# Layer 0's edge sums of a four-layer graph network: a block for each tile of 128 edges, loads from two queues

## The chip, the cores and the metric

The kernel runs on one core of a Trainium2 chip. The metric is device time in microseconds (us) for the whole program, which is one launch; smaller is better. The core has five engines that run side by side and meet through semaphores: PE (TensorE, matmuls), DVE (VectorE), ACT (ScalarE), POOL (GpSimd) and SP (SyncE), which here only issues transfers.

## The reference

A graph has 6,250 nodes with 128 features and 200,000 edges sorted by their target `dst`. Four message-passing layers follow one another, each with a residual. The change touches only the edge sum of the first and the making of its lists:

```python
def _L0_gnn_ref(x, edge_index, W1, b1, W2, b2):
    src, dst = edge_index[0], edge_index[1]
    agg = jax.ops.segment_sum(x[src], dst, num_segments=6250)
    h = (1.0 + EPS) * x + agg
    return jax.nn.relu(h @ W1 + b1) @ W2 + b2
...
    x = x + _L0_gnn_ref(h, edge_index, L0_gnn_W1, L0_gnn_b1, L0_gnn_W2, L0_gnn_b2)
```

The targets are drawn as 6250 times the square of a uniform number, so that the first nodes have many more edges than the last. Layers 1 to 3 (a filter network with softplus, an attention layer with a segment softmax, a relation layer with another softmax) have edge stages of their own.

## The kernel before

Nodes are cut into 49 windows (`WIN`) of `P` = 128, edges into **groups** of `GE` = 512 = `KG` (4) tiles of 128. A group belongs to one window. The windows' edges fill at most `NG` = 440 groups, and all loops over groups run 440 times. Where a window's last group has fewer than 512 edges left, the rest of its tiles hold edges of the next windows, and their one-hot rows are zero.

**The lists.** `pack_edges` makes on DVE, for two orders of the edges, the window, the first edge and the base (128 times the window) of each group: counts per window, running sums (`scan`), and a comparison of each group's number with the running sums. SP writes the lists to DRAM and reads them back: `glist` (numbers) onto one partition, `gbase` broadcast to all, where DVE derives `gsame` (is this group's window that of the group before?).

**The edge sum of layer 0** is `segment_sums(k, 0)`, lines 1164 to 1320. For each group:

- SP `load`: waits on `summed`, reads the first edge's number (L1161), and loads the 512 edge records with one DMA of 128 partitions x 64 bytes (L1194). It leads the sum by one group (`LOAD` = 1).
- POOL `gather`: waits for the records and for `summed`, and issues four indirect DMAs (L1216); each fetches for 128 edges the source node's row as three bf16 parts, 768 bytes, into `sum_far`.
- DVE `one_hot`: the target within the window (L1233) and four one-hot tiles of 128x128 (L1237), one group ahead.
- PE `total`: 12 matmuls (L1301), four tiles by three parts, all accumulated into one block of 128x128 of PSUM bank a % 2. It waits for the one-hots, for the add of two groups before (two banks) and for the four gathers.
- DVE `add`: one operation (L1245) that takes the running block times `gsame` plus the bank's block.
- ACT `keep`: waits for the add, reads the window's number (L1157) and copies the running block to that window's place in `acc` (L1283); a later copy for the same window overwrites it.
- DVE `rank`: a piece of other work over 1,570 columns, one of four operations (L1251, L1254, L1258, L1261) in every second group.

Rows and gathered rows live in `U` = 4 slots, so that load and gather of group a wait until PE's sum of group a - 4 has been counted. Each engine runs its own instructions in program order; `skewed` writes that order, with the leads as offsets, in a loop of eight groups a turn. The semaphore `summed` is increased by PE's last matmul of a group, and `added` by the add, `kept` by the copy.

Later stages, which the change leaves alone, have the same shape with more work per group: the message sum (`sum_messages`), the attention stage (gathers at L1705) and the relation stage (gathers at L1943), all with eight slots and longer leads.

## Time and profile before

| what | us |
|---|---|
| median of three runs | 13527.47 |
| lowest and highest run | 13472.64, 13547.69 |
| the profiled execution, whole | 13520.75 |
| its span | 13518.5 |
| stage of layer 0's edge sums in it (269.0 to 3062.5) | 2793.5 |

The profile is one execution; starts are microseconds from the span's start. In rows of instructions, "[4.04 <-DMA x]" is the time that the engine was idle before the row and what its wait ended with. A name with q (SPq, ACTq) is the engine's sequencer, where transfers are issued and numbers read into registers; such instructions are not counted as busy. "issue" is idle time with nothing waited for. "remote" is a wait whose releaser the profile can't name. "x12" is the number of instructions in a row.

### The profile page before, as it was taken

How to read it: one execution, taken by the hardware profiler on the slowest of the kernel's cores; microseconds unless marked ns; L12 is line 12 of the kernel's file. 1: busy time of each engine (PE TensorE's matmuls, PEld its weight loads, DVE VectorE, ACT ScalarE, POOL GpSimd, SP SyncE). 2: the span in 40 equal slices, each digit the busy share in tenths (PEclk: the TensorE clock that was granted, in tenths of full speed). 3: DMA queues.
4: the chain of work that ended last, by engine and by line, in shares of the span. 5: the costliest groups of instructions: out<-in, count | busy, mean ns of one | idle time of the engine just before them, and what ended most of it. 6: DMA issues, size and time to landing. Idle time of an engine off the chain costs nothing. (4 is left out here: it accounts for less than half of the span.)

```text
span 13518.5 us, 245976 instructions
## 1 busy us (share of the span) xinstructions
PE 8019.6 (59%) x56223; PEld 6235.5 (46%) x56224; DVE 7891.0 (58%) x29629; ACT 4807.1 (36%) x9638; POOL 6957.0 (51%) x7329
## 2 busy tenths in 40 slices
PE   0222222226777767677885666666662878777776
PEld 0111111114444444444774655555552656555555
DVE  6333333335555555555776777777777666666665
ACT  2000000005555555555324555555552222222222
POOL 1656565553555555555214555555552555555553
PEclk9955555557676676666998888888886777777777
DMA  3222222221111111111651111111111222222221
GB/s 110 64 63 63 63 64 63 64 63 36 42 42 41 41 40 40 38 40 29 180 179 47 49 49 49 49 48 49 48 50 31 49 51 51 51 51 51 50 51 44
DMA packets 1025180, 771.96 MB, mean 57 GB/s; under 512 B 698606, under 2 KB 868943, under 8 KB 1024742
## 3 DMA queue, kind: packets, MB, share of 16 engines
q0 software_dynamic: 272816, 573.30, 15.3%
q1 hardware_dynamic: 752309, 198.07, 6.6%
q8 instruction: 18, 0.29, 0.0%
q14 instruction: 37, 0.30, 0.0%
HBM read 585.49 MB, written 155.84 MB: 55 GB/s over the span
## 5 line engine op out<-in xcount | busy, mean ns | idle before, releaser
L1492 POOL DMA_INDIRECT message_records<-f_msg,f_index x1760 | 1761.0, 1001 | 1683.8 <-DVE f_msg L1552 1162.7
L1705 POOL DMA_INDIRECT a_far<-node_table,a_rows x1784 | 1685.5, 945 | 1537.4 <-PE banks L1867 479.5
L1943 POOL DMA_INDIRECT r_far<-node_table,r_rows x1784 | 1704.4, 955 | 1467.9 <-remote 505.4
L1216 POOL DMA_INDIRECT sum_far<-split_table,sum_rows x1760 | 1668.8, 948 | 1205.1 <-issue 625.9
L1301 PE MATMUL banks<-sum_far,sum_hot 128*128 128x128 bf16 x5280 | 627.3, 309 | 2252.5 <-DVE sum_hot L1237 1260.2
L1301 PEld LDWEIGHTS banks<-sum_far,sum_hot 128*128 128x128 bf16 x5280 | 528.7, 143 | 2351.0 <-issue 1345.6
L1245 DVE SCALAR_TENSOR_TENSOR sum_cur<-sum_cur,gsame,banks 128x128 f32<-128x128 f32 x440 | 151.7, 345 | 1805.9 <-remote 1376.6
L1532 DVE SCALAR_TENSOR_TENSOR f_soft<-f_pos_part,f_logs 128x512 f32<-128x512 f32 x442 | 304.5, 689 | 1401.5 <-remote 763.9
L1283 ACT ACTIVATE acc<-sum_cur 128x128 f32 x440 | 136.1, 309 | 2704.8 <-DVE sum_cur L1245 1853.0
L1620 PE MATMUL banks<-f_attr_t,w_f 20*128 20x512 f32 x890 | 722.0, 902 | 560.7 <-ACT f_attr_t L1564 278.8
L1612 PE MATMUL banks<-w_W_f,f_soft 128*128 128x128 f32 x3528 | 757.3, 357 | 239.3 <-issue 236.9
L2032 ACT ACTIVATE r_keys<-banks 128x1024 bf16<-128x1024 f32 x446 | 455.2, 1021 | 1056.6 <-remote 886.3
L2072 PE MATMUL banks<-near,r_hot_t 128*128 x5328 | 767.0, 257 | 81.4 <-issue 70.5
L1564 ACT ACTIVATE f_attr_t<-banks 20x512 f32<-20x512 f32 x446 | 260.3, 584 | 1523.5 <-remote 1353.1
L1859 PE MATMUL banks<-ident,a_prob_t 128*128 128x128 f32 x1768 | 325.3, 312 | 798.7 <-ACT a_prob_t L1811 788.5
L2091 PE MATMUL banks<-r_far,r_share 128*128 128x129 f32 x3528 | 718.7, 362 | 120.7 <-DVE r_share L2010 69.9
L1612 PEld LDWEIGHTS banks<-w_W_f,f_soft 128*128 128x128 f32 x3528 | 640.3, 259 | 277.0 <-issue 275.5
L2091 PEld LDWEIGHTS banks<-r_far,r_share 128*128 128x128 f32 x3528 | 604.9, 257 | 158.8 <-DVE r_share L2010 86.0
L1867 PE MATMUL banks<-a_far,a_prob 128*128 128x129 f32 x3528 | 621.8, 332 | 84.2 <-ACT a_prob L1789 71.0
L1632 PE MATMUL banks<-near,f_hot_t 128*128 x5292 | 563.2, 272 | 151.1 <-issue 145.2
L1806 ACT ACTIVATE a_keys<-banks 128x512 bf16<-128x512 f32 x446 | 266.3, 597 | 1026.9 <-remote 585.2
L1867 PEld LDWEIGHTS banks<-a_far,a_prob 128*128 128x128 f32 x3528 | 560.7, 241 | 127.7 <-ACT a_prob L1789 78.4
(350 smaller groups left out, 21274.5 us busy)
## 6 DMA issues: line engine op xcount, KB each, us to landing
m_rows<-message_records SPq DMA_DIRECT2D x223, 264.0 KB
m_rows<-message_records POOLq DMA_DIRECT2D x223, 264.0 KB
acc<-a_cur SPq DMA_DIRECT2D x440, 65.0 KB
acc<-r_cur SPq DMA_DIRECT2D x440, 65.0 KB
a_far<-node_table,a_rows POOLq DMA_INDIRECT x1784
r_far<-node_table,r_rows POOLq DMA_INDIRECT x1784
sum_far<-split_table,sum_rows POOLq DMA_INDIRECT x1760
message_records<-f_msg,f_index POOLq DMA_INDIRECT x1760
```

Of the source, the lines that this page charges most:

```text
L1216: pool.indirect_dma_start(far[:, u, q, :], None, k.table3[:, :], bass.IndirectOffsetOnAxis(ap=rows[:, u, q, C_SRC:C_SRC + 1].bitcast(I32), ...
L1301: last = nc.tensor.matmul(k.psum[a % 2][:, 0:D], hot[:, u, q, :], rhs, start=q == 0 and part == 0, stop=q == KG - 1 and part == (2 if o == ...
L1492: pool.indirect_dma_start(k.mrec[:, :], bass.IndirectOffsetOnAxis(ap=index[:, u, q:q + 1], axis=0), msg[:, u, q, :], None, bounds_check=ED ...
L1612: last = nc.tensor.matmul(filter_ps[b][:, q * D:(q + 1) * D], soft[:, b, q * P:(q + 1) * P], w_f2[:, :], start=True, stop=True)
L1620: nc.tensor.matmul(hidden_ps[b], k.w_f1[:, :], attr_t[:, b, :], start=True, stop=True).then_inc(hidden_ready, 1)
L1632: last = nc.tensor.matmul(ps[:, q * D:(q + 1) * D], hot_t[:, q * P:(q + 1) * P], k.near[:, w, part * D:(part + 1) * D] .rearrange("p a d - ...
L1705: pool.indirect_dma_start(far[:, u, q, 0:D], None, k.table[:, :], bass.IndirectOffsetOnAxis(ap=rows[:, u, q, C_SRC:C_SRC + 1].bitcast(I32) ...
L1867: last = nc.tensor.matmul(sum_ps[b][:, 0:D + 1], prob[:, b, q * P:(q + 1) * P], far[:, u, q, 0:D + 1], start=q == 0, stop=q == KG - 1)
L1943: pool.indirect_dma_start(far[:, u, q, 0:D], None, k.table[:, :], bass.IndirectOffsetOnAxis(ap=rows[:, u, q, M_DST - M_SRC:M_DST - M_SRC + ...
L2032: nc.scalar.activation(keys[:, a % 2, :, :], key_ps, ACT.Copy).then_inc(keys_taken, 1)
L2072: nc.tensor.matmul(near_ps[b][:, span], hot_t[:, h, span], k.near[:, w, part * D:(part + 1) * D] .rearrange("p a d -> p (a d)"), start=par ...
L2091: last = nc.tensor.matmul(sum_ps[b][:, 0:D + 1], share[:, b, q, :], far[:, u, q, 0:D + 1], start=q == 0, stop=q == KG - 1)
```

## The change

Layer 0 gets a function of its own, `sum_targets`, in place of `segment_sums(k, 0)`. Its unit is the **tile** of 128 edges of one window: at most `NT` = 1612 tiles, each with its own window, first edge and base. Four tiles in a row of the list make a group, whatever their windows, so there are `NTG` = 403 groups. The lists are made in `pack_edges` with some 30 more linked DVE operations of the same kinds, go out in three more DMAs, and are read at the start of the stage: the numbers onto one partition, the base as [128, 1664] broadcast, from which DVE makes `same`.

- Slots for rows and gathered rows: `S` = 8 in place of 4; the gathered rows lie in memory of a later stage (`k.near`). One-hots keep four slots. Leads: loads 7, gathers 4, one-hots 2, sums 1, adds 0 (before: 1, 0, 1, 0, 0).
- SP loads tiles 0 and 1 of a group, ACT tiles 2 and 3: four DMAs of 128 partitions x 16 bytes (L1235) in place of one.
- PE puts each tile's three matmuls into a block of its own of the bank, 12 per group as before.
- DVE chains four adds per group (L1306), each waiting for the last through `carried`.
- ACT copies four blocks per group to `acc` (L1350), with four window numbers read (L1232). In its loop, the load of group a + 7 (which waits for the sum of a - 1) stands ahead of the copies of group a.
- `skewed` takes `total`, with the three groups that are no whole turn of eight written out behind the loop.

```diff
+NT = EDGES // P + WIN + 1
+NTG = (NT + KG - 1) // KG
+TQ = 13
+NTL = P * TQ
...
+                dve.wait_ge(numbered, 2)
...
+                upto = scan(dve, groups, WIN)
+                link(dve, nc.vector.tensor_tensor(tpast[:, :, :], ti[:, :].unsqueeze(2).to_broadcast(spread),
+                                                  upto[:, 0:WIN].unsqueeze(1).to_broadcast(spread), ALU.is_ge))
+                link(dve, nc.vector.tensor_reduce(tw[:, :], tpast[:, :, :], AX, ALU.add))
...
+                sp.wait_ge(listed, 1)
+                for i, t in enumerate((tw_i, ts_i)):
+                    sp.dma_start(k.tile_lists[i, :].rearrange("(p q) -> p q", p=P), t[:, :]).then_inc(list_out, 16)
+                sp.dma_start(k.tile_bases[0, :].rearrange("(p q) -> p q", p=P), tb[:, :]).then_inc(list_out, 16)
...
-def skewed(eng, *stages, counts=None, turn=U):
+def skewed(eng, *stages, counts=None, turn=U, total=NG):
...
+    whole = total // turn * turn
+    with eng.Fori(0, whole, turn) as g:
         if counts:
             counts.turn()
         for u in range(turn):
             for lead, stage in stages:
                 stage(g, u + lead)
+    for n in range(whole, total):
+        for lead, stage in stages:
+            stage(0, n + lead)
...
-    LOAD, HOT, SUM, ADD = 1, 1, 0, 0
...
+    LOAD, GATHER, HOT, SUM, ADD = 7, 4, 2, 1, 0
+    S, H = 2 * U, U
...
+        far = k.near[:, 0:S * KG, :].rearrange("p (u q) c -> p u q c", q=KG)
...
+        def numbers(eng, which, g, a, first, n, most):
+            place = tiles[0:1, which, bass.ds((g + a) * KG + first, n)]
+            return nc.values_load_multi_w_load_instructions(place, engines=[eng.engine], min_val=0, max_val=most)[1]
+
+        def load_tile(eng, e0, u, q):
+            eng.dma_start(rows[:, u, q, :], k.erec[bass.ds(e0, P), :]).then_inc(loads_in[u], 16)
...
+                sp.dma_start(tiles[:, :, :], k.tile_lists.rearrange("(a i) g -> a i g", a=1)).then_inc(listed, 16)
+                sp.dma_start(base[:, :], k.tile_bases.broadcast_to([P, NTL])).then_inc(listed, 16)
+                sp.wait_ge(listed, 32)
...
                 def load(g, a):
-                    sp.wait_ge(summed, now(g, s_sum + a + 1))
-                    e0 = first_edge(sp, k, o, g + a)
-                    sp.dma_start(rows[:, a % U, :, :].rearrange("p q c -> p (q c)"),
-                                 records[bass.ds(e0, GE), :].rearrange("(p q) c -> p (q c)", q=KG))\
-                        .then_inc(k.rows_in[a % U], 16)
-                skewed(sp, (LOAD, load), counts=now, turn=2 * U)
...
+                    wait(sp, now, summed, g, a, S)
+                    sp.sem_inc(k.loading, 1)
+                    for q, e0 in enumerate(numbers(sp, 1, g, a, 0, 2, EDGES + EP)):
+                        load_tile(sp, e0, a % S, q)
+                skewed(sp, (LOAD, load), counts=now, turn=S, total=NTG)
...
+                    pool.wait_ge(loads_in[u], slot_count(now, g, a, 16 * KG, S, s_load[u]))
+                    wait(pool, now, summed, g, a, S)
+                    pool.sem_inc(k.begun, 1)
+                    for q in range(KG):
+                        pool.indirect_dma_start(
+                            far[:, u, q, :], None, k.table3[:, :],
+                            bass.IndirectOffsetOnAxis(ap=rows[:, u, q, C_SRC:C_SRC + 1].bitcast(I32), axis=0))\
+                            .then_inc(gathered[u], 16)
+                skewed(pool, (GATHER, gather), counts=now, turn=S, total=NTG)
...
+                    dve.wait_ge(loads_in[u], slot_count(now, g, a, 16 * KG, S, s_load[u]))
+                    wait(dve, now, summed, g, a, H)
+                    nc.vector.tensor_tensor(rel[:, h, :], rows[:, u, :, C_DST].bitcast(I32), base[:, bass.ds((g + a) * KG, KG)],
...
-                    dve.wait_ge(summed, now(g, s_sum + U + a + 1))
-                    dve.wait_ge(added, now(g, s_add + 2 + a))
-                    dve.wait_ge(kept, now(g, s_kept + a + 1))
-                    nc.vector.scalar_tensor_tensor(cur[:, u, :], cur[:, (u - 1) % U, :], k.gsame[o][:, bass.ds(g + a, 1)],
-                                                   k.psum[a % 2][:, 0:D], ALU.mult, ALU.add).then_inc(added, 1)
+                    wait(dve, now, summed, g, a)
+                    dve.wait_ge(kept, now(g, KG * (a + 1), KG))
+                    for q in range(KG):
+                        past = cur[:, u, q - 1, :] if q else cur[:, (u - 1) % U, KG - 1, :]
+                        dve.wait_ge(chained, now(g, KG * a + q + 1, KG))
+                        last = nc.vector.scalar_tensor_tensor(cur[:, u, q, :], past, same[:, bass.ds((g + a) * KG + q, 1)],
+                                                              k.psum[a % 2][:, q * D:(q + 1) * D], ALU.mult, ALU.add)
+                        last.then_inc(chained, 1)
+                    dve.wait_ge(chained, now(g, KG * a + KG + 1, KG))
+                    dve.sem_inc(added, 1)
...
+                act.wait_ge(listed, 32)
+                act.sem_inc(kept, KG * U)
+
+                def load(g, a):
+                    wait(act, now, summed, g, a, S)
+                    act.sem_inc(k.loading, 1)
+                    for q, e0 in enumerate(numbers(act, 1, g, a, 2, 2, EDGES + EP)):
+                        load_tile(act, e0, a % S, 2 + q)
 
                 def keep(g, a):
-                    act.wait_ge(added, now(g, s_add + 2 + a + 1))
+                    wait(act, now, added, g, a)
                     act.sem_inc(k.loading, 1)
-                    act.wait_ge(kept, now(g, s_kept + U + a))
-                    act.sem_inc(k.loading, 1)
-                    w = window(act, k, o, g + a)
-                    nc.scalar.activation(k.acc[:, w, 0:D], cur[:, a % U, :].unsqueeze(1), ACT.Copy).then_inc(kept, 1)
-                skewed(act, (ADD, keep), counts=now, turn=2 * U)
+                    for q, w in enumerate(numbers(act, 0, g, a, 0, KG, WIN)):
+                        act.wait_ge(kept, now(g, KG * U + KG * a + q, KG))
+                        nc.scalar.activation(k.acc[:, bass.ds(w, 1), 0:D], cur[:, a % U, q, :].unsqueeze(1), ACT.Copy).then_inc(kept, 1)
+                skewed(act, (LOAD, load), (ADD, keep), counts=now, turn=S, total=NTG)
...
                 def total(g, a):
-                    u = a % U
-                    pe.wait_ge(onehot_ready, now(g, s_hot + a + 1))
-                    pe.wait_ge(added, now(g, s_add + a + 1))
-                    if o == 0:
-                        pe.wait_ge(k.pool_done[u], now(g, s_pool[u] + 16 * KG * (a // U + 1), 16 * KG // U))
+                    u = a % S
+                    wait(pe, now, onehot_ready, g, a)
+                    wait(pe, now, added, g, a, 2)
+                    pe.wait_ge(gathered[u], slot_count(now, g, a, 16 * KG, S, s_gather[u]))
                     for q in range(KG):
-                        for part in range(3 if o == 0 else 1):
-                            rhs = far[:, u, q, part * D:(part + 1) * D] if o == 0 else rows[:, u, q, 0:D]
-                            last = nc.tensor.matmul(k.psum[a % 2][:, 0:D], hot[:, u, q, :], rhs,
-                                                    start=q == 0 and part == 0, stop=q == KG - 1 and part == (2 if o == 0 else 0))
+                        for part in range(3):
+                            last = nc.tensor.matmul(k.psum[a % 2][:, q * D:(q + 1) * D], hot[:, a % H, q, :],
+                                                    far[:, u, q, part * D:(part + 1) * D], start=part == 0, stop=part == 2)
                     last.then_inc(summed, 1)
-                skewed(pe, (SUM, total), counts=now, turn=2 * U)
+                skewed(pe, (SUM, total), counts=now, turn=S, total=NTG)
```

ACT's program in one pass of the loop. Before, one copy of `sum_cur` into `acc` for each group:

```order
L1280 REGISTER_ALU [waits added]
L1157 ISA [waits kept]
L1157 TENSOR_LOAD glist
L1157 ISA x2
L1283 ISA
L1283 ACTIVATE acc<-sum_cur 128x128
```

Now, for each group, from the load of two tiles' records (`t_rows`) to the second of the four copies:

```order
L1232 ISA [waits summed]
L1232 TENSOR_LOAD t_tiles
L1232 ISA x4
L1235 ISA
L1235 DMA t_rows<-edge_records 128x4
L1235 ISA
L1235 DMA t_rows<-edge_records 128x4
L1163 REGISTER_ALU
L1232 ISA [waits added]
L1232 TENSOR_LOAD t_tiles
L1232 ISA x8
L1349 REGISTER_ALU
L1350 ISA [waits kept]
L1350 ACTIVATE acc<-t_cur 128x128
L1349 REGISTER_ALU
L1350 ISA [waits kept]
L1350 ACTIVATE acc<-t_cur 128x128
```

ACT now waits for two semaphores in turn, `summed` for the load and `added` for the copies, and issues two DMAs per group where it issued none.

DVE's program at the head of the loop. Before, from the one-hots of one group to its add:

```order
L1232 REGISTER_ALU [waits rows_in1]
L1233 ISA [waits summed]
L1233 TENSOR_SCALAR sum_rel<-sum_rows,gbase 128x4
L1237 TENSOR_SCALAR sum_hot<-iota_b,sum_rel 128x128 [waits rel_ready]
L1237 TENSOR_SCALAR sum_hot<-iota_b,sum_rel 128x128 x3
L1242 REGISTER_ALU
L1245 REGISTER_ALU [waits kept,added,summed]
L1245 SCALAR_TENSOR_TENSOR sum_cur<-sum_cur,gsame,banks 128x128
```

Now, the adds of one group, behind the same five operations for the one-hots:

```order
L1302 ISA [waits summed]
L1305 REGISTER_ALU [waits kept]
L1306 ISA [waits carried]
L1306 SCALAR_TENSOR_TENSOR t_cur<-t_cur,t_same,banks 128x128
L1305 REGISTER_ALU
L1306 ISA [waits carried]
L1306 SCALAR_TENSOR_TENSOR t_cur<-t_cur,t_same,banks 128x128
L1305 REGISTER_ALU
L1306 ISA [waits carried]
L1306 SCALAR_TENSOR_TENSOR t_cur<-t_cur,t_same,banks 128x128
L1306 ISA [waits carried]
L1306 SCALAR_TENSOR_TENSOR t_cur<-t_cur,t_same,banks 128x128
```

One add of 128x128 has become four, in a chain.

## Rows read from the trace of the kernel before

**Rows 1.** The page: busy tenths of POOL in 40 slices of the span
```profile
POOL 1656565553555555555214555555552555555553
```
**Rows 2.** Busy time in stretches: us, then PE, PEld, DVE, ACT, POOL (count), PEclk, DMA, GB/s
```profile
269.00:3062.50 2793.50, 627.32 (x5280) 528.74 (x5280) 960.61 (x2870) 136.10 (x440) 1668.78 (x1760) 0.59 0.25 64
...
7226.00:10233.00 3007.00, 1991.66 (x16197) 1781.77 (x16195) 2183.41 (x8316) 1671.57 (x4379) 1654.38 (x1752) 0.86 0.19 49
10487.00:13406.00 2919.00, 2318.73 (x16635) 1719.24 (x16633) 1837.94 (x10074) 852.46 (x1749) 1674.18 (x1752) 0.73 0.22 51
```
**Rows 3.** One line's instructions, POOL's gathers (L1216): duration, and what ended idle time
```profile
L1216 POOL DMA_INDIRECT sum_far<-split_table,sum_rows x1760: 940/947/1295, 272.7 to 3048.8; - x196
...
  issue: 625.9, 1651
  DMA sum_rows<-edge_records: 419.3, 74
  PE banks L1301: 152.3, 33
  remote: 7.6, 2
```
**Rows 4.** Timeline of layer 0's stage from 1548 to 1563 us, all engines
```profile
1548.28 1.44 PE L1301 MATMUL banks<-sum_far,sum_hot 128*128 128x128 bf16 x12 [3.65 <-DMA sum_far<-split_table,sum_rows]
...
1555.52 0.95 POOL L1216 DMA_INDIRECT sum_far<-split_table,sum_rows  x1 [0.30 <-issue]
1559.41 0.35 DVE L1245 SCALAR_TENSOR_TENSOR sum_cur<-sum_cur,gsame,banks 128x128 f32<-128x128 f32 x1 [12.43 <-remote]
...
1560.72 0.31 ACT L1283 ACTIVATE acc<-sum_cur 128x128 f32 x1 [13.75 <-DVE sum_cur L1245]
1561.13 0.34 DVE L1245 SCALAR_TENSOR_TENSOR sum_cur<-sum_cur,gsame,banks 128x128 f32<-128x128 f32 x1
...
1562.51 0.95 POOL L1216 DMA_INDIRECT sum_far<-split_table,sum_rows  x1 [6.04 <-DMA sum_rows<-edge_records]
```
**Rows 5.** Count of matmuls (L1301) from the stage's start to 1559.00: us, PE, PEld
```profile
269.00:1559.00 1290.00, 287.67 (x2424) 242.58 (x2424) 0.69 0.25 64
```
**Rows 6.** Count of DVE's adds (L1245) in the same stretch: us, DVE
```profile
269.00:1559.00 1290.00, 69.00 (x200) 0.69 0.25 64
```
**Rows 7.** One line's instructions, DVE's add (L1245): what ended DVE's idle time before it
```profile
  remote: 1376.6, 144
```
**Rows 8.** Timeline at the start of the attention stage, POOL and DVE
```profile
7212.79 0.94 POOL L1705 DMA_INDIRECT a_far<-node_table,a_rows  x1 [0.30 <-issue]
...
7216.85 0.70 DVE L1740 TENSOR_TENSOR banks<-banks,a_far 128x512 f32<-128x512 f32 x1 [30.41 <-remote]
...
7226.75 0.94 POOL L1705 DMA_INDIRECT a_far<-node_table,a_rows  x1 [13.01 <-PE banks L1867]
```
**Rows 9.** Instructions of sequencers and ACT's copy: duration min/median/max in ns
```profile
L1194 SPq DMA_DIRECT2D sum_rows<-edge_records x441: 4/333/1397, 270.0 to 3045.6; - x147
...
L1157 ACTq FUSED_REGOPS  x1760: 42/100/173, 283.2 to 7015.5; - x196
...
L1157 ACTq TENSOR_LOAD <-glist x880: 272/279/492, 283.3 to 7015.1; - x176
...
L1283 ACT ACTIVATE acc<-sum_cur x440: 309/309/311, 284.2 to 3056.8; 128x128 f32 x147
```
**Rows 10.** Timeline of the stage's first loads and first gather
```profile
270.00 4.29 SPq L1194 DMA_DIRECT2D sum_rows<-edge_records  x4
...
272.68 1.14 POOL L1216 DMA_INDIRECT sum_far<-split_table,sum_rows  x1 [96.78 <-issue]
```
**Rows 11.** The lists: DVE's operations for one of them, and the load of `gbase` (timeline)
```profile
149.90:158.96 9.06, 0.00 (x0) 0.00 (x0) 7.78 (x39) 0.00 (x0) 0.00 (x0) 1.00 0.02 1
...
162.12 0.34 SPq L478 DMA_DIRECT2D gbase<-group_bases  x1
165.63 0.06 DVE L464 MEMSET gsame<- 128x1 f32 x1 [6.68 <-DMA gbase<-group_bases]
```

More of the change, by code:

```diff
@@ L245, in program @@
         publish(k, k.hs, True)
-        segment_sums(k, 0)
+        sum_targets(k)
         sum_nodes(k)
@@ new lines, in load @@
+                    wait(sp, now, summed, g, a, S)
[3 more added lines that the diff above has]
+                skewed(sp, (LOAD, load), counts=now, turn=S, total=NTG)
+                sp.wait_ge(pos_ready, 1)
+                for half in range(2):
+                    sp.dma_start(k.epos[half * EP:(half + 1) * EP, :].rearrange("(p j) a -> p (j a)", p=P), pos_i[:, :])\
+                        .then_inc(pos_out, 16)
@@ new lines, in _, with gather @@
+                sp.wait_ge(pos_out, 32)
+                for u in range(S):
+                    sp.wait_ge(loads_in[u], s_load[u] + len(range(u, NTG + LOAD, S)) * 16 * KG)
+            @block.gpsimd
+            def _(pool):
+                now = Counts(pool)
+                def gather(g, a):
+                    u = a % S
[8 more added lines that the diff above has]
+                skewed(pool, (GATHER, gather), counts=now, turn=S, total=NTG)
@@ L1222, in _ @@
             @block.vector
             def _(dve):
[L1224 to L1225 removed]
                 now = Counts(dve)
[L1229 to L1235 removed]
+                k.link(dve, nc.vector.memset(cur[:, :, :, :], 0.0))
@@ L1303, in total @@
                     last.then_inc(summed, 1)
-                skewed(pe, (SUM, total), counts=now, turn=2 * U)
-    k.since.passed(NG + HOT, rel_ready, onehot_ready)
-    k.since.passed(NG + U, summed, kept)
-    k.since.passed(NG + 2, added)
-    per_slot(k.since, k.rows_in, 16, LOAD)
-    if o == 0:
-        per_slot(k.since, k.pool_done, 16 * KG, 0)
+                skewed(pe, (SUM, total), counts=now, turn=S, total=NTG)
+    for u in range(S):
+        k.since.passed(16 * KG * len(range(u, NTG + LOAD, S)), loads_in[u])
+        k.since.passed(16 * KG * len(range(u, NTG + GATHER, S)), gathered[u])
```

124 lines of the change are left out of this document (62 added, 62 removed).

## The prediction

> **What bounds the kernel now.** I read the slices first: the change touches layer 0's edge sums, in which POOL is the busiest engine for a fifth of the span [rows 1]. The table of stretches puts that stage at 2793.5 us, with POOL busy for 1668.8, DVE for 960.6, PE for 627.3 and ACT for 136.1 [rows 2]. So no engine is full, and the question is what POOL waits for. Its own line answers: 1,760 gathers of 0.95 us, and between them 625.9 us of "issue", of which 96.8 precede the first gather [rows 3, 10]; the remaining 529 us over 440 groups are 1.20 us per group. Four gathers take 4 x 0.95 + 1.20 = 5.0 us. On top POOL waits 419.3 us for the records, 152.3 for the banks and 7.6 for others: 579 us in 109 pauses, 5.3 us each and one per 4.04 groups [rows 3]. 440 x 5.0 + 579 = 2779, which with the start and the end is the stage.
>
> **Why POOL pauses** is the main reading. The timeline shows PE finishing a group's matmuls at 1548.28 + 1.44 = 1549.72 [rows 4]. DVE's add for it, which waits only for that and for an add and a copy long done, starts at 1561.13, and the add of the group before at 1559.41 [rows 4]. The counts agree: at 1559.00 PE had run 2,424 matmuls, 202 groups of 12, and DVE 200 adds [rows 5, 6]. So the increment that PE's last matmul makes reaches the others up to 10 us late. In the stretch POOL starts its last gather at 1555.52 and ends it at 1556.47; then comes 2.9 us of nothing, DVE's add, and at 1562.51 POOL again, after 6.04 us [rows 4]. The attention stage starts the same way: POOL gathers without a break until 7213.7, DVE's wait of 30.41 us ends at 7216.85, 3.1 us behind the last gather, and POOL goes on at 7226.75, after 13.01 us, though its slots are eight [rows 8]. DVE waited 1376.6 us for "remote" before its add, 144 times [rows 7]: a releaser that left no record in time. My reading: while gathers follow one another at 1.25 us, PE's increments are held back; when POOL runs out of slots, they arrive after about 3 us; then records are loaded and the next run begins. Before, a run is 4.04 groups, the four slots, and a pause is 5.3 us.
>
> Where the profile gives an end time to a matmul, the Trainium skill (Perfetto Trace Analysis, section on the Tensor Engine instruction) warns that it is an estimate, and that the semaphore goes out only when PSUM has acknowledged. By that rule the 10 us could be PSUM's; that the increment then comes about 3 us behind POOL's last gather, twice, speaks for POOL. The sum is the same by either.
>
> **The change, part by part.**
>
> *Fewer groups.* 403 for 440 in the loop; POOL also gathers the 4 ahead of it, 407 in all. With nothing but this, 33 x 6.31 (= 2776 from the first gather to the last, over 440) = 208 us less.
>
> *Deeper slots.* A run of gathers was bounded by 4 slots and can now be up to 8 groups. It doesn't reach 8 for sure: PE waits for the add two groups back, the adds wait for the late increments, so at the end of a run up to six gathered groups have not been summed, and their slots come free one after another, while POOL has started again. Bounds: 4.04 as now, and 8. I take 6.5, above the middle, since some increments also come within a run.
>
> *The pause* has a new chain behind it. The increment arrives 3 us after the last gather as now; since longer runs hold more of them (the wait in the attention stage ended after 3.1 us with 8 slots [rows 8]), I allow 3 to 5. Then:
> - SP's half of the records: about 1.4 us for a list read and two issues (0.33 us each [rows 9], and up to 1.4 where a row is stretched), and 272.68 - 270.00 - 0.33 = 2.35 us from the end of an issue to POOL's start [rows 10]. With the increment 6.8 to 8.8 us.
> - ACT's half stands behind the copies of the last group in its order. Those wait for four adds, 4 x 0.35 + the waits between = 1.7 us; then for a read of four numbers (0.28 + four times some 0.25 of register work, from 0.10 per operation [rows 9]) and four copies of 0.31 [rows 9] with a wait after each, together 3.3 us. Between add and copy one number took 1560.72 - 1559.41 - 0.35 = 0.96 us [rows 4], so this isn't too much. Then 1.4 us of issues and 2.35: 3 + 1.7 + 3.3 + 1.4 + 2.35 = 11.8, up to 13.8.
>
> Before, the same sum was 2.9 + 3.1 = 6.04 in the example and 5.3 on average, since some pauses start with an increment on its way. When several increments arrive together ACT's later loads do hide behind gathers, so I take 9.5, between SP's path and ACT's. That is 9.5 / 6.5 = 1.46 us per group where it was 5.3 / 4.04 = 1.31.
>
> *PE.* 12 matmuls per group as before, 1.44 us [rows 4], under POOL's 5.0. *DVE.* It was 960.6 / 440 = 2.18 us per group [rows 2]; three more adds of 0.35 and their waits make 3.6, under POOL. If POOL's cover were gone (all waits away), DVE would still fit. *ACT.* One copy and one number become 3.3 + 1.4 + waits = 5.1 us per group, just over POOL's 5.0 and under my pace; nothing is hidden there for long, see below.
>
> *Start and lists.* Making the tile lists: another set like the 39 operations of 9.06 us [rows 11], on the path, +9. At the stage's start a broadcast load 3.6 times as wide as `gbase`, which took 165.63 - 162.12 = 3.5 us [rows 11], bound 3.5 to 12.6, and a comparison on DVE: I take +6. The clearing of `acc` on DVE is beside the first gathers. Three list DMAs and POOL's second `iota`: below 1 us.
>
> **Sum.** Pace 5.0 + 1.46 = 6.46 us. 407 x 6.46 = 2629, + 4 from the stage's start to the first gather as before + 6 for the loads, and nothing at the end, since the last four groups gathered are never summed: 2639. Against 2793.5 that is -154; with the lists +9, **-145**. The profiled execution was 13520.75, so 13,376; the median lies 6.7 above it: 13,383 us. I say **13,380**. Its own range: pace 6.2 to 6.87 (the attention stage's 3007 / 438 [rows 2], where the same eight slots stand over twice the DVE work) gives 407 x -0.26 = -106 and 407 x +0.41 = +167, so 13,275 to 13,550.
>
> **Rivals.**
>
> *A: the eight slots swallow the late increments.* Within a run some increments do come, or POOL would never get beyond its slots; if they come at least every 10 us, eight slots never run dry. Then POOL is the bound, 407 x 5.0 = 2035 + 27 for start and end = 2062; -731 + 9: 12,805 us. With a residual of 0.6 per group 13,050. For it: 109 pauses, each one as the four slots ran out. Against it: the attention stage and the relation stage, with eight slots, hold 6.87 and 6.66 us [rows 2], and DVE's 30 us without an increment [rows 8]. But their groups carry 5.0 us (2183 / 438) and 4.2 us of DVE and 4.5 and 5.3 us of PE, so part of that pace is their own.
>
> *B, the slower side: ACT is held back as SP is.* SP's instructions, a 0.33 us issue for one, take up to 1.4 us [rows 9] in this stage, and ACT's do not (0.49 at most), but ACT issued no DMA here. If it is the issuing that exposes a sequencer, ACT's 5.1 us get longer: 4 of its 29 sequencer instructions per group held by one step of 0.65 us make it 5.1 + 2.6 = 7.7. Then ACT is the bound for every group: 407 x 7.7 = 3134 + 10; +350 + 9: 13,887 us. It decides from about 6.85 us of ACT per group on, where 407 x 6.85 meets the old stage.
>
> *C: the small loads queue.* The stage's first four loads took 4.29 us, (4.29 - 0.33) / 3 = 1.3 us apart with a number read for each [rows 10]. If four DMAs of one group come in at that distance, a pause grows by 3 x 1.3 = 4.0, or 0.61 per group: pace 7.07, +248: 13,630. Two issuers speak against the full price. The Trainium skill (DMA: Bandwidth & Descriptors, Rules for kernel authors) tells to coalesce, as below 64 KB one pays mostly overhead, and says in Issuing engines are not separate DMA queues that two engines only save issue time. By that rule the four transfers of 2 KB cost more than the one of 8 KB, which is this rival; no row of before has loads from two queues here.
>
> That the loop isn't shortened at all can be left out: its length is a constant, 403.
>
> **Chances.** Main .50, A .25, B .13, C .12. A measurement here tells about 0.5%, 67 us, from no change. Faster by more than that, below 13,460: A, and .35 of main: .60. Within: .12 of main and .05 of C: .17. Slower: B, .07 of C, .03 of main: .23. The range takes in A at 12,805 and C, and leaves out B: 12,800 to 13,750.
>
> **What would show it.** In the profile after: the stage's length near 2640; some 60 pauses of POOL of 9 to 10 us, each some 6.5 groups apart, ending with the records and not with the banks (if pauses are fewer than 20, A). DVE's add starting 3 to 5 us after POOL's last gather, with matmuls long done. ACT's issues as the last loads of a group before POOL restarts; ACT's issue rows with a median of 0.35 us or less (if they reach 0.7 to 1.4, B). The four loads of a group landing within 1 us of their issues (if they land 1.3 apart, C). I am wrong as a whole if PE's increments are late for a reason that isn't POOL, such as the load on the banks: three accumulations per block in place of twelve would then change the lateness itself.

## The result, and the profile after

The changed kernel took 13,692.55 us at a median of four runs (13,688.97 to 13,706.16), the kernel before beside it 13,529.56 (13,472.64 to 13,547.69): a ratio of 1.013, 95% interval 1.0099 to 1.016. I had forecast 13,380, faster. The time lies inside the stated range; the sign is wrong.

One thing must be known to read the numbers below: the same kernel before, run beside the experiments, took 10,374 to 10,385 us on six occasions and 13,502 and 13,665 us on two others; two of the chips showed both. I call them the **prompt** and the **late** condition, by what the traces show to differ between them. The result, and the profile on which the prediction was made, are late. In the late condition whole times also drift: the kernel before took 13,473 to 13,665 us.

The page of the changed kernel, late: POOL's busy tenths over the span (as rows 1).

```profile
POOL 1555555553555555555323555555552555555553
```

The stage of layer 0 in the same kernel: us, then busy PE, PEld, DVE, ACT, POOL (count), PEclk, DMA share, GB/s (as rows 2).

```profile
275.00:3198.00 2923.00, 583.06 (x4848) 484.73 (x4848) 1316.78 (x3845) 498.38 (x1612) 1547.56 (x1628) 1.00 0.25 57
```

The stage took 2923.0 us where it was 2793.5: +129.5. The stretch ahead of it is 6.0 longer (lists), the rest of the kernel, which is unchanged, took 10,506.5 against 10,456.0, +50.5; together 186, the difference of the two spans. The last part is within what this kernel varies between runs; the first two are the change. PE's granted clock was full in the stage (1.00, 2.4 GHz) where it had been 0.59 on average, mostly at the lower level of 1.2 GHz, and the stage was longer all the same: PE was no bound before or after.

POOL's gathers (L1269), what ended its idle time (as rows 3):

```profile
L1269 POOL DMA_INDIRECT near<-split_table,t_rows x1628: 942/949/2067, 285.1 to 3184.3; - x181
its engine sat idle before it (us, times) until:
  DMA t_rows<-edge_records: 904.7, 184
  issue: 493.5, 1416
  PE banks L1365: 56.2, 28
```

(2899.2 us over 1,627 intervals: 7.13 us per group.) Taking off the 101.8 us ahead of the first gather, POOL waited 859 us in 211 pauses of 4.1 us, one per 1.9 groups. Before it was 109 pauses of 5.3, one per 4.0 [rows 3]. So pauses became twice as frequent, where I had forecast fewer. They end with the records, as I had said. DVE's adds tell who is late now. DVE's add (L1306), what ended DVE's idle time before it (as rows 7):

```profile
  ACT acc L1350: 1179.6, 334
```

DVE may not overwrite a slot of the running block before ACT has copied it, four groups on. It waited for ACT for 1,180 us, where before it waited for no copy at all. ACT itself hardly waited: what ended its idle time before its copies (L1350) was almost always nothing at all.

```profile
  issue: 2219.3, 426
```

Counting instruction by instruction, ACT's sequencer stood for 81 of 2,899 us in front of its semaphore waits, and SP's for 1,280. So ACT had become the pace. The timeline of two groups in the middle of the stage:

```profile
1546.94 1.61 ACT L1350 ACTIVATE acc<-t_cur 128x128 f32 x4 [3.56 <-issue]
...
1551.20 0.95 POOL L1269 DMA_INDIRECT near<-split_table,t_rows  x1 [0.30 <-issue]
...
1553.49 0.84 ACTq L1235 DMA_DIRECT2D t_rows<-edge_records  x2
1556.05 1.61 ACT L1350 ACTIVATE acc<-t_cur 128x128 f32 x4 [7.49 <-issue]
1556.68 0.95 POOL L1269 DMA_INDIRECT near<-split_table,t_rows  x1 [4.53 <-DMA t_rows<-edge_records]
1557.79 1.82 DVE L1306 SCALAR_TENSOR_TENSOR t_cur<-t_cur,t_same,banks 128x128 f32<-128x128 f32 x4 [4.42 <-ACT acc L1350]
```

Between two sets of copies ACT issues two loads; POOL restarts 3.2 us after the first of them, DVE adds when the four copies that began at 1556.05 are done. What ACT does between 1549.13 and 1553.49 is the heart of the matter. These are its sequencer's instructions (start and duration in us, from the trace):

```
1549.13 0.015 EVENT_SEMAPHORE (summed)
1549.15 0.013 FUSED_REGOPS
1549.19 0.704 TENSOR_LOAD t_tiles
1550.59 0.015 FUSED_REGOPS
1550.61 0.015 SEQ_ASSERT
1552.02 0.018 FUSED_REGOPS
1552.04 0.707 SEQ_ASSERT
1553.44 0.006 FUSED_REGOPS
1553.49 0.334 DMA_DIRECT2D t_rows
```

An assert that takes 0.018 us elsewhere takes 0.707, and register operations stand 1.41 us apart. POOL's last gather ran from 1551.20 to 1552.15, and from 1553.44 on ACT's instructions have their usual lengths again. From the first gather to the last, 727 of ACT's 13,471 sequencer instructions took over 0.6 us; in the kernel before, none of 3,658.

### The profile page after: what moved, and what is told of

Same layout as the page of the kernel before. It is cut to its first block and busy times, and to the rows that moved or that the text cites. A ratio compares the mean times of both kernels' runs of the same rounds, so it can differ in the third digit from the quotient of the medians.

```text
span 13704.5 us, 262447 instructions
## 1 busy us (share of the span) xinstructions
PE 7988.4 (58%) x55791; PEld 6205.3 (45%) x55792; DVE 8249.8 (60%) x30630; ACT 5172.2 (38%) x10810; POOL 6831.9 (50%) x7198
## 5 line engine op out<-in xcount | busy, mean ns | idle before, releaser
L1269 POOL DMA_INDIRECT near<-split_table,t_rows x1628 | 1547.6, 951 | 1454.4 <-DMA t_rows<-edge_records 904.7
L1365 PE MATMUL banks<-near,t_hot 128*128 128x128 bf16 x4848 | 583.1, 309 | 2409.1 <-DVEq L1310 1643.4
L1365 PEld LDWEIGHTS banks<-near,t_hot 128*128 128x128 bf16 x4848 | 484.7, 142 | 2507.4 <-issue 2503.6
L1350 ACT ACTIVATE acc<-t_cur 128x128 f32 x1612 | 498.4, 309 | 2475.6 <-issue 2219.3
L1306 DVE SCALAR_TENSOR_TENSOR t_cur<-t_cur,t_same,banks 128x128 f32<-128x128 f32 x1612 | 559.7, 347 | 1423.7 <-ACT acc L1350 1179.6
L2098 ACT ACTIVATE banks<-banks 128x512 f32<-128x512 f32 x444 | 260.4, 586 | 933.9 <-remote 821.2
```

The costliest lines, as they stand in the source:

```text
L1269: pool.indirect_dma_start(far[:, u, q, :], None, k.table3[:, :], bass.IndirectOffsetOnAxis(ap=rows[:, u, q, C_SRC:C_SRC + 1].bitcast(I32), ...
L1306: last = nc.vector.scalar_tensor_tensor(cur[:, u, q, :], past, same[:, bass.ds((g + a) * KG + q, 1)], k.psum[a % 2][:, q * D:(q + 1) * D], ...
L1350: nc.scalar.activation(k.acc[:, bass.ds(w, 1), 0:D], cur[:, a % U, q, :].unsqueeze(1), ACT.Copy).then_inc(kept, 1)
L1365: last = nc.tensor.matmul(k.psum[a % 2][:, q * D:(q + 1) * D], hot[:, a % H, q, :], far[:, u, q, part * D:(part + 1) * D], start=part == 0 ...
```

## The experiments

Nine kernels, four of them met in both conditions. Runs of the same kernel are told together. The table gives each run and the kernel before that was measured beside it; "per group" is POOL's mean distance between gathers, times four; "long" is the number of sequencer instructions over 0.6 us from the first gather to the last.

| kernel | condition | us | before | per group | long SP / ACT |
|---|---|---|---|---|---|
| before | late | 13,521 | | 6.31 | 554 / 0 |
| changed | late | 13,693 | 13,530 | 7.13 | 631 / 727 |
| one load on ACT (g2) | late | 13,584 | 13,502 | 6.86 | 1095 / 949 |
| all loads on SP (i3) | late | 13,791 | 13,665 | 7.02 | 1094 / 862 |
| one-window groups, 8 slots (j1) | late | 13,688 | 13,665 | 6.27 | 647 / 528 |
| before (f1) | prompt | 10,377 | 10,383 | 5.01 | 0 / 0 |
| changed (f2) | prompt | 10,308 | 10,383 | 5.19 | 1 / 1 |
| two gathers left out (g1) | prompt | 10,309 | 10,378 | 5.19 | 1 / 1 |
| all loads on SP (e1) | prompt | 10,237 | 10,382 | 5.02 | 1 / 0 |
| one copy (e3) | prompt | 10,237 | 10,382 | 5.02 | 0 / 1 |
| one-window groups, 8 slots (e5) | prompt | 10,421 | 10,382 | 5.02 | 0 / 0 |
| the same, load on ACT (h3) | prompt | 10,426 | 10,377 | 5.02 | - / 0 |
| before, load on ACT (e2) | prompt | 11,028 | 10,382 | 6.48 | - / 0 |

(g1 has two gathers to a group: 2108.7 us over 406.5 groups. The first row is the profiled execution of the median 13,527. "Changed, late", e1 and e5 are medians of four, four and five runs, with their intervals in the text; all other rows are single runs. The 13,665 beside i3 and j1 is one and the same execution.)

As whole times drift in the late condition, the stretch from the first gather to the last is the firmer number there, though it too is one trace each: 2776.1 us before, 2899.2 changed, 2789.2 in g2, 2855.1 in i3, 2783.5 in j1.

### All loads on SP

```diff
-                    for q, e0 in enumerate(numbers(sp, 1, g, a, 0, 2, EDGES + EP)):
+                    for q, e0 in enumerate(numbers(sp, 1, g, a, 0, KG, EDGES + EP)):
...
-                skewed(act, (LOAD, load), (ADD, keep), counts=now, turn=S, total=NTG)
+                skewed(act, (ADD, keep), counts=now, turn=S, total=NTG)
```

> The changed kernel with all four tile loads of a group issued by SP; ACT only copies. Theory 1 (ACT, once it issues transfers, is held back in steps of 0.7 and 1.4 us while POOL gathers, and its 7.2 us per group are the pace): ACT's sequencer rows in layer 0's stage have no step of 0.7 us any more, the pace falls to 5.8 to 6.6 us per group, time 13,230 to 13,520 us. Theory 2 (the four copies and four numbers per group are too much for ACT's place in the chain, whoever issues the loads): the pace stays near 7.2 us, time 13,650 to 13,720 us. A third outcome, slower than 13,720 us, would say that SP with four issues per group is held back even more.

> As before for this kernel. Beside a kernel before of 13,500 us: no steps among ACT's instructions and 13,470 to 13,560 us by theory 1; above 13,650 us if SP is the one held.

The first runs were in the prompt condition: 10,237 against 10,382, ratio 0.9864 (0.9848 to 0.9881), four runs; repeats gave 10,239, 10,239, 10,245 and 10,235. There POOL gathers without a pause:

```profile
L1269 POOL DMA_INDIRECT near<-split_table,t_rows x1628: 942/946/2155, 286.3 to 2328.6; - x181
its engine sat idle before it (us, times) until:
  issue: 495.3, 1626
```

In the late condition (i3) the same kernel took 13,791 against 13,665, one run each: slower by 126 us, and 79 us more than before from the first gather to the last. "Above 13,650 if SP is the one held" came true. DVE's one-hots (L1292) show it; the first row is how often and for how long DVE waited for records, the others SP's and ACT's durations for the numbers (L1232), min/median/max in ns:

```profile
  DMA t_rows<-edge_records: 1199.9, 367
```

```profile
L1232 SPq FUSED_REGOPS  x2040: 2/147/1402, 281.1 to 3144.6; - x186
L1232 ACTq FUSED_REGOPS  x2012: 3/147/997, 299.6 to 3126.2; - x183
L1232 SPq SEQ_ASSERT  x1640: 2/18/1392, 281.3 to 3144.8; - x183
L1232 ACTq SEQ_ASSERT  x1612: 3/18/727, 300.5 to 3127.0; - x180
```

One pass of SP for four loads takes 3.6 us undisturbed and took 10.3 in the middle of a run of gathers (1548.26 to 1558.52). SP's sequencer stood for 5 of 2,855 us in front of its waits, ACT's for 623: here SP was the pace. And ACT, which issues no transfer in this kernel, still has 862 long instructions. **Theory 1, that issuing transfers is what exposes ACT, has fallen.**

### One load on ACT, three on SP

> The changed kernel with three of a group's loads on SP and one on ACT in place of two and two. ACT's undisturbed pass gets shorter by one number (0.17 us) and one issue (0.52 us), from 5.14 to 4.45 us, under POOL's 5.0. Beside a kernel before of 10,380 us: if ACT's pass is the bound and nothing else of the two-queue form costs anything, 10,235 to 10,245 us, as with all loads on SP. Beside 13,520 us: by theory 1 ACT is still held in steps while it issues at all, pace 6.3 to 6.9 us, 13,330 to 13,570 us; all loads on SP would do better than that.

This run was in the late condition: 13,584 against 13,502. Its pace of 6.86 us is in the range I gave, its time 14 us above the upper end, and all loads on SP did not do better, as I had expected, but worse. By the paces, the two-and-two split is the slowest (7.13), three-and-one the least slow (6.86), all on SP between (7.02). Of 2,789 us ACT's sequencer stood for 156 in front of its waits and SP's for 605, so ACT was still the slower one. Work moved from one held sequencer to the other; no split brings the pace near 6.31.

### The kernels before and after, again

> The kernel before, unchanged, for its profile beside the next three. In the first profile it took 13,521 us; beside the four experiments so far it took 10,382 us at a median, 23% less. Two theories of that gap. Theory 3 (late increments): what differs is only whether PE's increments and the sequencers' steps come late while POOL gathers; where they do, layer 0's stage has 109 to 116 pauses and takes about 2,794 us, where they don't it has none and takes 440 x 5.02 = 2,209 us plus 15. Theory 4 (clock or memory speed): single operations, POOL's gathers of 0.95 us or the matmuls, have other durations. The total will be near 13,520 or near 10,380 us; nothing between, by theory 3.

> The changed kernel, unchanged. Theory 3: where PE's increments are late (the kernel before near 13,520 us), 13,690 us as measured first; where they are not (before near 10,380 us), ACT fits under POOL, the 33 groups fewer give 33 x 5.02 = 166 us back less 9 for the lists and some 12 at the start: 10,225 to 10,250 us, faster than before by 1.3%. If ACT were too slow for its place whatever the increments do, it would be slower than before in both.

f1 came out as theory 3 had it: no pause in layer 0's stage, single gathers of the same length (a median of 946 ns against 947). The stage is 576 us of the 3,143 between the two conditions; the other 2,566 lie behind it, in stages whose pace I have not taken apart. The stage of f1 (as rows 2) and what ended POOL's idle time in it:

```profile
268.00:2485.50 2217.50, 635.32 (x5280) 527.82 (x5280) 968.03 (x2871) 136.06 (x440) 1667.66 (x1760) 1.00 0.31 80
```

```profile
L1216 POOL DMA_INDIRECT sum_far<-split_table,sum_rows x1760: 942/946/1141, 271.6 to 2474.2; - x196
its engine sat idle before it (us, times) until:
  issue: 632.8, 1760
```

PE's increments were not late either: 0.02 us after the modelled end of the matmul at most. In the late trace an increment's record lies up to 10.4 us behind the latest matmul end before it, which is a lower bound, as two increments can arrive together: matmuls that ended at 1544.63 and 1549.72 were followed by increments at 1559.30 and 1559.42. So four slots are enough where nothing is held. The changed kernel was faster there, by 0.7%, but 58 us above the upper end of what I expected. Its ACT, in two passes of the loop with nothing held (f2):

```profile
1002.05 1.61 ACT L1350 ACTIVATE acc<-t_cur 128x128 f32 x4 [3.65 <-PE banks L1365]
...
1003.79 1.82 DVE L1306 SCALAR_TENSOR_TENSOR t_cur<-t_cur,t_same,banks 128x128 f32<-128x128 f32 x4 [2.09 <-ACT acc L1350]
1004.66 0.85 ACTq L1235 DMA_DIRECT2D t_rows<-edge_records  x2
...
1007.19 1.61 ACT L1350 ACTIVATE acc<-t_cur 128x128 f32 x4 [3.52 <-issue]
```

From copies to copies it is 5.14 us with no wait in it, and POOL needs 5.01. ACT's sequencer didn't stand in front of a wait for over 0.12 us once between the first gather and the last, in f2 as in g1 below.

### Two gathers left out

```diff
-                    for q in range(KG):
+                    for q in range(2):
                         pool.indirect_dma_start(
...
-                                                    far[:, u, q, part * D:(part + 1) * D], start=part == 0, stop=part == 2)
+                                                    far[:, u, q % 2, part * D:(part + 1) * D], start=part == 0, stop=part == 2)
```

> The changed kernel with two of POOL's four gathers per group left out (PE multiplies the one-hots of tiles 2 and 3 with the rows of tiles 0 and 1). ACT's program is untouched. POOL then needs 2.5 us per group and can't be the bound. If ACT's own row of instructions is what sets the pace (5.14 us per group read between two passes of its loop where nothing is late), the pace stays at 5.15 to 5.3 us and the time, beside a kernel before of 10,380 us, is 10,290 to 10,320 us, as with four gathers (10,308). If POOL's gathers were the bound there, the stage falls by up to half: below 10,000 us. Beside a kernel before of 13,520 us: if ACT's steps of 0.7 us come from POOL's gathers, half of them are gone, pace 5.3 to 6.3 us; if they have another source, it stays at 7.2.

10,309.3 against 10,308.4 with all four gathers, one run each: POOL's work was halved and the time didn't move. In the prompt condition ACT's pass sets the changed kernel's pace, not POOL's gathers. The run was not in the late condition, so that half of the expectation stays untried.

### One copy per group

```diff
-                    for q, w in enumerate(numbers(act, 0, g, a, 0, KG, WIN)):
-                        act.wait_ge(kept, now(g, KG * U + KG * a + q, KG))
...
+                    for q, w in enumerate(numbers(act, 0, g, a, KG - 1, 1, WIN)):
+                        act.wait_ge(kept, now(g, U + a))
```

> The changed kernel with one copy and one window number per group on ACT in place of four (copies of tiles 0 to 2 are left out); its two loads per group stay. Theory 1: ACT stays held back, but has some 2 us less to do per group: the pace falls from 7.2 to 5.8 to 6.6 us, time 13,130 to 13,500 us, with the steps of 0.7 us still in ACT's rows. Theory 2: the pace falls as well, but to POOL's and the slots' bound, 5.0 to 5.6 us, below 13,100 us.

> The changed kernel with one copy and one number per group on ACT in place of four (copies of tiles 0 to 2 left out), its two loads kept. Beside 13,500 us: theory 1 expects the steps to stay and the pace to fall from 7.2 to 5.8 to 6.5 us, 13,130 to 13,420 us, since ACT has 10 instructions fewer that can be held. If the four copies are what counts, not the holding, no steps are needed to explain it and the time is below 13,100. Beside 10,380 us: 10,237 us.

Both runs (e3, h4) were in the prompt condition, 10,237 and 10,239 us, the time of all loads on SP. Either way of shortening ACT's pass below POOL's 5.0 gives back the same 70 us. Of the late condition these runs say nothing, and the two theories of the expectations were about that alone.

### Groups of one window with eight slots

The load, one-hot, add and copy of the kernel before, 440 groups, with the changed kernel's slots, leads and semaphores.

```diff
-                    for q, e0 in enumerate(numbers(sp, 1, g, a, 0, 2, EDGES + EP)):
-                        load_tile(sp, e0, a % S, q)
-                skewed(sp, (LOAD, load), counts=now, turn=S, total=NTG)
+                    e0 = first_edge(sp, k, 0, g + a)
+                    sp.dma_start(rows[:, a % S, :, :].rearrange("p q c -> p (q c)"),
+                                 k.erec[bass.ds(e0, GE), :].rearrange("(p q) c -> p (q c)", q=KG)).then_inc(loads_in[a % S], 16)
+                skewed(sp, (LOAD, load), counts=now, turn=S, total=NG)
```

> Groups of 512 edges of one window, one load by SP, one add and one copy per group as in the kernel before (440 groups), but with the eight slots and the leads 7, 4, 2, 1, 0 of the changed kernel; the tile lists are still made (9 us). It shows what slots and leads alone do. If eight slots swallow PE's late increments (rival A of the prediction), POOL is the bound with 5.0 to 5.3 us per group: 12,960 to 13,090 us. If pauses stay as in the main forecast, 5.3 us each for 6.5 groups, 5.8 us per group: 13,290 to 13,380 us. If deeper slots change nothing, 13,500 to 13,560 us.

> Groups of one window, eight slots, long leads, one load by SP. Beside a kernel before of 13,500 us: SP has 7 instructions per group that can be held in place of the changed kernel's 17 on SP and 29 on ACT. If the number of SP's and ACT's instructions is what made the changed kernel slow, this one has pauses no oftener than before: 13,290 to 13,400 us if longer runs save pauses, 13,480 to 13,560 if they don't. If it lies above 13,650 too, the eight slots themselves do harm. Beside 10,380 us: 10,421 us, nothing new.

Prompt (e5): 10,421 against 10,382, ratio 1.004 (1.0026 to 1.0054), and 10,424 and 10,421 in repeats. Of the 39 us the lists are 9, and four groups gathered ahead that nobody sums 20 (16 gathers of 1.25 us); some 10 are not accounted for. The three outcomes of the expectation all presumed the late condition, so this run decided none of them.

Late (j1): 13,688 us, one run; the nearest kernel before is the 13,665 measured beside i3. From the first gather to the last it is 2783.5 us against 2776.1, with four groups more gathered. **Eight slots with the long leads gain nothing by themselves.** POOL's gathers:

```profile
L1267 POOL DMA_INDIRECT near<-split_table,t_rows x1776: 940/946/1345, 279.3 to 3062.8; - x198
its engine sat idle before it (us, times) until:
  issue: 524.6, 1676
  DMA t_rows<-edge_records: 489.4, 65
  PE banks L1348: 148.3, 26
  remote: 30.9, 9
```

Counted in one way for both (gaps of over 2.2 us between starts, less the 1.25 of a gather): 99 pauses of 5.61 us, 555 us, where the kernel before had 116 of 4.92, 571 us. Runs got longer and pauses longer with them. The timeline shows such a run:

```profile
1542.16 0.34 DVE L1298 SCALAR_TENSOR_TENSOR t_cur<-t_cur,gsame,banks 128x128 f32<-128x128 f32 x1
...
1558.14 0.35 DVE L1298 SCALAR_TENSOR_TENSOR t_cur<-t_cur,gsame,banks 128x128 f32<-128x128 f32 x1 [12.88 <-issue]
1558.59 1.44 PE L1348 MATMUL banks<-near,t_hot 128*128 128x128 bf16 x12 [14.45 <-issue]
...
1565.33 0.35 DVE L1298 SCALAR_TENSOR_TENSOR t_cur<-t_cur,gsame,banks 128x128 f32<-128x128 f32 x1 [5.88 <-remote]
1565.49 0.94 POOL L1267 DMA_INDIRECT near<-split_table,t_rows  x1 [3.97 <-remote]
```

PE stands still for 14.45 us, since it may be only two groups ahead of the adds and the adds wait for its increments. While POOL works through its slots nothing else moves, so the groups gathered meanwhile have all to be summed afterwards, and the slots come free at PE's and DVE's pace. ACT, with one copy and one number per group and no transfer, has 528 long instructions, against none in the kernel before, whose ACT program is nearly the same. But it is no bound here: its sequencer stood for some 1,630 of 2,783 us in front of its waits, and SP's for 1,370.

### The load on ACT, with four and with eight slots

```diff
-                skewed(act, (ADD, keep), counts=now, turn=2 * U)
+                skewed(act, *(((LOAD, load),) if o == 0 else ()), (ADD, keep), counts=now, turn=2 * U)
```

> The kernel before, with the one load per group of layer 0 issued by ACT ahead of its copy in place of by SP; nothing else. Theory 1: ACT's list reads and register operations, which never took over 0.5 us before, are now spread by steps of 0.7 and 1.4 us, some hundreds of them in the stage; as ACT has little to do per group, the time moves by less than 1%, 13,450 to 13,650 us. Theory 2: no such steps in ACT's rows, time 13,470 to 13,550 us.

> The same as the last, with the group's one load issued by ACT ahead of its copy. ACT's undisturbed pass is 2.6 us per group, far under POOL's 5.0. Beside 13,500 us: theory 1 expects hundreds of steps of 0.7 and 1.4 us among ACT's instructions, which hardly show without the load; the time moves by less than 60 us, as 2.6 us leave room. If ACT has no steps, theory 1 falls. Beside 10,380 us: 10,415 to 10,430 us.

Both runs were prompt, so neither says anything on theory 1. With the four slots and the lead of one group of the kernel before (e2; the edit above), the load in ACT's program costs 646 us, far more than I had expected:

```profile
L1217 POOL DMA_INDIRECT sum_far<-split_table,sum_rows x1760: 940/946/1188, 271.0 to 3119.8; - x196
its engine sat idle before it (us, times) until:
  DMA sum_rows<-edge_records: 673.5, 299
```

With eight slots and a lead of seven (h3) the same move costs 5 us (10,426 against the 10,421 of h2, measured beside it). A load on ACT is dear only where slots and lead are short; the two were changed together. This is what they do buy the changed kernel.

The runs f3, f4, h1, h2, i1 and i2 repeated the kernels of e1 and e5 in the prompt condition and agree with them within 0.1%.

### When the sequencers are held

From the late traces, the share of sequencer instructions that took over 0.6 us, by the time since POOL's run of gathers began (a run ends where two starts are over 2.2 us apart), and while POOL stood:

```
us since start    0-2   2-4   4-6   6-8   8-10  POOL standing
before     SP     0.03  0.09  0.28  0.68  0.19  0.03
before     ACT    0     0     0     0     0     0
changed    SP     0.01  0.09  0.09  0.32  0.45  0.02
changed    ACT    0     0     0.03  0.43  0.43  0.02
i3         SP     0     0.11  0.36  0.53  0.53  0.03
i3         ACT    0     0     0.19  0.66  0.54  0.04
j1         SP     0.03  0.20  0.41  0.64  0.60  0.02
j1         ACT    0     0.06  0.19  0.54  0.66  0
```

From some 4 to 6 us into a run of back-to-back gathers on, mostly a third to two thirds of what SP and ACT execute takes over 0.6 us, whatever the instruction; ACT in the kernel before is the exception. In the prompt condition POOL gathers for 2,000 us without a break, and hardly one instruction is long: the gathers are not enough to hold a sequencer.

Two more things can be read from these traces. First, the transfers that bring in instructions are not what SP and ACT lack: between 329 and 3,064 us the late trace of the kernel before has none, and the late one of the changed kernel has none between 371 and 3,158. Second, the late traces lack many of the records of DVE's and ACT's increments (327 are there for DVE's 440 adds in the kernel before, and all 440 in f1), though none of their instructions. So whether the taking of the profile has a part in the late condition is an open question; no run on record tests it.

## Why the prediction was wrong, step by step

- **What bounds the kernel before: right in the late condition.** PE's increments come late while POOL gathers. That this isn't the rule of the kernel but of a condition, I couldn't see from one trace; f1 shows that the gathers alone don't cause it. Where nothing is held, POOL's 5.01 us per group is the pace with four slots.
- **"I take 6.5" groups per run: the first step that failed.** With only slots and leads changed (j1) a run came to 4.5 groups (444 over 99), but the pauses grew from 4.92 to 5.61 us, and the pace went from 6.31 to 6.27. Of a longer hold I had made no more than 3 to 5 us for the increment. What I left out of the price is what I had written one paragraph earlier: PE may be two groups ahead of the adds, so during a run it does nothing.
- **ACT "just over POOL's 5.0 and under my pace": the step that turned the sign.** The 5.1 us were right for an ACT that isn't held: 5.14 in f2, and g1 shows that it is the bound there. But I took them for the late condition too, though SP's rows with 1.4 us stood before me [rows 9], and gave the case that ACT is held only .13. It was held, and as it stood for only 81 us in front of its waits, its pass was the pace: 7.13 us per group for my 6.46. The pauses came every 1.9 groups and took 4.1 us, not every 6.5 groups and 9.5 us: 2.1 us per group for my 1.46.
- **Rival B named the right mechanism with the wrong reason and price.** ACT became the bound, DVE waited 1,180 us for its copies, and 6.85 us as the point from which the change loses was right: at 6.86, g2 took 13 us more than the kernel before from the first gather to the last, and began 13 later. I had 7.7 for 7.13, and 13,887 for 13,693. The reason I gave, that issuing transfers exposes a sequencer, is refuted by i3 and j1.
- **Rival A** describes the prompt condition, but not for its reason: no increments are late there. Its 12,805 us are of no use, since the stages behind layer 0 move with the condition as well (7,890 us in f1, 10,456 before).
- **Rival C**: no sign of it. With four small loads per group on SP, POOL has no pause in the prompt condition; the rule that transfers under 64 KB cost mostly overhead (the Trainium skill, DMA: Bandwidth & Descriptors, Rules for kernel authors) showed here only as sequencer time, 0.52 us per issue. The Trainium skill (DMA: Bandwidth & Descriptors, Issuing engines are not separate DMA queues) calls this time usually small relative to the transfer. Here it was 0.52 us beside the 2.35 from an issue to POOL's start [rows 10], smaller as the page says; yet two issues were 1.04 of ACT's 5.14 us, and moving them to SP with their two numbers gave back the 70 us between f2 and e1.
- **Small terms.** The stage began 6.0 us later, for 9 forecast; its start to the first gather took 10.1 us, for 10. "Nothing at the end" was wrong: 13.7 us from the last gather's start to the stage's end, since ACT has three groups' copies and loads to go through. Before it was 13.7 too, by another way, the writing of the edges' positions.
- **The gain of 37 groups fewer is real**: in the prompt condition, with ACT out of the way (e1), 145 us, 1.4%; it is 33 gathered groups of 5.02 (166) less lists and start. That this is the -145 of my forecast is chance: mine was made of other terms. It is the fastest kernel found there of those that leave no work out; in the late condition none of the versions tried beats the kernel before.

**What stays open.** Why a program runs in one condition or the other: chips 4 and 9 gave both, so it isn't the chip alone. Why ACT was not held in the kernel before, in some 750 instructions at over 6 us into a run, while it was in j1 with nearly the same program. And what holds the sequencers: transfers of instructions are ruled out by the traces, the rest is not known. One copy per group, half the gathers, and a load on ACT in the kernel before were never run in the late condition.

## What to carry to other kernels

Count the sequencer instructions per turn of every engine that reads numbers or issues transfers, not its busy time: an ACT that is 23% busy in f2 was the bound, at 5.14 us of registers, numbers, issues and small copies. Deeper slots don't help where the consumer stands still for as long as the producer runs; ask what the consumer does meanwhile. And when a profile shows one sequencer's plain instructions taking 0.7 us, reckon that the instructions a change puts on another one can be held as well, and measure in both conditions, since the sign can differ: 1.3% slower (four runs each) and 0.7% faster (one run each) here.

## What the runs showed of the hardware

The same program took some 13,500 and 10,380 us, with single operations of equal length (gathers 947 and 946 ns at the median, matmuls 309 and 309 ns on average). In the late condition, many of SP's and ACT's plain instructions took 0.7 us or stood 1.4 us apart, from some 4 us into a run of back-to-back indirect DMAs of POOL until shortly after its end, with ACT in the kernel before excepted. PE's increments came at least 10.4 us after the matmuls' modelled end at the latest (at least 23.8 with eight slots), while those of DVE and ACT, as far as recorded, came within 0.01 us. PE's granted clock in layer 0's stage was 0.59 on average in the kernel before when late (between 1.2 and 2.4 GHz) and 1.00 when prompt, and 1.00 in the changed kernel in both. It had no share in the stage's time: PE was busy for 627 and 635 us with the same 5,280 matmuls.
